# Two-layer gated cross-attention and mixture of experts: the first expert part cut to 16 tiles, and layer 0's experts started beside the last attention iterations

## The chip, the cores and the metric

The kernel runs on one core of a Trainium2 chip. The metric is the device time of one execution in microseconds (us), lower is better. The core has a matrix engine (PE), three elementwise engines (DVE, ACT, POOL) and a queue engine (SP) that only issues transfers; each engine works through its own list of instructions in order, and they meet at semaphores. A bank is one of eight 128 x 512 float32 blocks of PSUM, the memory that PE writes to.

## What is computed

Two layers over x, 128 sequences of 64 tokens of width 128 (8192 tokens, 64 tiles of 128). Each layer adds a cross-attention and then a mixture of experts, both gated by a tanh. What the change touches is in layer 0: a 16-head attention, then top-2 routing over 8 experts of hidden width 512.

```python
x = x + jnp.tanh(g_xattn[0]) * _L0_xattn_ref(_layernorm(x, axis=-1), ctx_1024, ctx_1024, ...)
x = x + jnp.tanh(g_ffn[0]) * _L0_ffn_ref(_layernorm(x, axis=-1), ...)
x = x + jnp.tanh(g_xattn[1]) * _L1_xattn_ref(_layernorm(x, axis=-1), ctx_1024, ctx_1024, ...)
x = x + jnp.tanh(g_ffn[1]) * _L1_ffn_ref(_layernorm(x, axis=-1), ...)

def _L0_ffn_ref(x, Wg, bg, W1, b1, W2, b2):      # E = 8, K = 2, H = 512
    scores = jax.nn.softmax(xt @ Wg + bg, axis=-1)
    topk_probs, topk_idx = jax.lax.top_k(scores, K)
    h = jnp.einsum('nd,edh->enh', xt, W1) + b1[:, None, :]
    h = jax.nn.gelu(h, approximate=False)
    eo = jnp.einsum('enh,ehd->end', h, W2) + b2[:, None, :]
    ...
    out = jnp.einsum('nk,nkd->nd', topk_probs, sel)
```

## The kernel before

**Stages.** Layer 0's attention is a software pipeline over NP = 32 pairs of tiles. Every engine has the loop `for p in range(NP + 3)`; iteration p scores pair p, turns the weights of pair p-1, attends for pair p-2 and writes the output of pair p-3. Its last three iterations (p = 32, 33, 34) only drain the pipeline. Then come layer 0's experts, layer 1's attention and layer 1's experts.

**Parts.** The expert layer works on three parts of the 64 tiles, `PARTS = ((0, 24), (24, 24), (48, 16))`. For each part DVE runs `route0(h)`, a generator of 12 steps (softmax, top 2, counts, where each token goes, which expert each block belongs to). DVE then normalises each tile's rows (`put_rows`), and POOL scatters them to DRAM with two indirect transfers for each tile (`put`), grouped by expert. A part becomes blocks of one expert each: first blocks of 256 rows, then 21 blocks of 128 rows. A part of 24 tiles has 17 + 21 blocks, one of 16 tiles 9 + 21, and all parts together have 43 large and 63 small blocks (NBL = 106). The rows of a large block, or of two small ones, are a unit.

**A block.** SP copies the expert's first weights (`fetch_weights`, three blocks ahead) and loads a unit's rows (`fetch_tokens`, three units ahead; it waits until the whole part is put). PE turns the rows (`turn0`, L837), multiplies by the first weights (`up0`, L847), ACT applies the gelu (L1752), PE multiplies by the second weights (`down0`, L857), DVE adds the bias (`add_bias0`, L1363) and SP stores the unit. When a part's last results are stored and every part's rows are put, POOL gathers the results, two indirect transfers a tile (`get`, L1960); DVE adds them to x (`combine`, L1371, in `earlier_part`), takes statistics, and POOL turns these into layer 1's means and scales (`moments1`). The gathers of the last part lie in layer 1's attention, where `LATER_BY` says how many tiles are combined by which group.

**Order around the change.** Part 0's `route0` begins at p = 17 and its scatters run from p = 23 to 34, two tiles an iteration; part 1's `route0` begins at p = 29; part 2's runs a step at a time between the first blocks of part 0. Scatters of parts 1 and 2 follow the loop, each tile behind its `put_rows`; DVE makes two rows a block while it is in part 0. Two fills of zeros (384 KB each, L459) go out in each iteration until 38 have. In the draining iterations PE, ACT and DVE also fold layer 1's weights (`turn_weights`, `output_bias(1)`, `multiply_weights`, `fold_weights`) in banks 0, 1 and 7. SP, behind all that it issues for the loop, fetches three blocks' weights, the two halves of `w2`, and the rows of units 0 to 2.

Of the kernel before, what the change touches and what calls it, by code (L numbers as in the profile page):

```python
# [13 lines left out]
ALU = mybir.AluOpType  # L14
# [6 lines left out]
P = 128  # L21
# [24 lines left out]
PARTS = ((0, 24), (24, 24), (48, 16))  # L46
# [39 lines left out]
PUT_FROM = 23  # L86
# [6 lines left out]


# [8 lines left out]
LATER_BY = (0, 1, 3, 5, 7, 9, 11, 13, 15, 16)  # L103
# [86 lines left out]
def build(nc, t_in, out):  # L190
    with ExitStack() as ctx:
# [30 lines left out]
        minus_half = sb("minus_half", [P, TS])  # L222
        ln_tmp = sb("ln_tmp", [P, 4, TS])
# [20 lines left out]
        xl_sb = sb("xl_sb", [P, P])  # L244
# [20 lines left out]
        scores_r = sb("scores_r", [P, 2, S])  # L265
        top = sb("top", [P, 2, 24])
        top_at = sb("top_at", [P, 2, 24], mybir.dt.uint32)
        tok = sb("tok", [P, 2, CAP])
        pair = sb("pair", [P, 2, CAP, 2])
        slot_sb = sb("slot_sb", [P, NCHUNK, NE, 2])  # L270
# [10 lines left out]


# [137 lines left out]
        def routing_start(h):  # L420
            return 2 * (sum(PARTS[h]) // TG - 1) + 7
# [8 lines left out]
        def sync_program(e):  # L430
# [46 lines left out]

            filling = fill()
            for p in range(NP):
                move_sums(p)  # L480
                if p % 4 == 2 and (p + 2) // 4 < NT // TS:
                    w.wait_ge(s_xl, (p + 2) // 4)
                    load_turned((p + 2) // 4)
                if p < NE:
                    load("w1", w1_sb[:, p, :], t_in["w1a"][:, p, :])
                for _ in range(2):
                    next(filling, None)
            for _ in filling:
                pass

# [28 lines left out]
            w.wait_ge(s_sc, NP)  # L519
            w.wait_ge(s_kx, NG)  # L520
            for b in range(AHEAD):
                fetch_weights(b)
            for i in range(2):
# [3 lines left out]
            for u in range(3):  # L527
                fetch_tokens(u)
# [50 lines left out]
        def tensor_program(e):  # L579
# [163 lines left out]
            def turn_weights():  # L743
                w.wait_ge(s_sub, NP)
                for n in range(3):
                    ins = e.transpose(banks[0][:, n * P:n * P + P], w_sb[:, 4 + n, :], ident[:])
                ins.then_inc(s_fm, 1)

            def multiply_weights():
# [4 lines left out]
                e.matmul(banks[1][:, 0:D], wk, wq, start=True, stop=True)  # L754
                e.matmul(banks[1][:, D:2 * D], wv, wo1_sb[:], start=True, stop=True)
                e.matmul(banks[1][:, 2 * D:2 * D + 1], wk, vec("bq1"), start=True, stop=True)
                e.matmul(banks[1][:, 2 * D + 1:2 * D + 2], wq, vec("bk1"), start=True, stop=True).then_inc(s_fm, 1)

            def multiply_bias():
                w.wait_ge(s_fs, 1)  # L760
                e.matmul(banks[0][:, 0:1], cen[:], fold1[:, 2:3], start=True, stop=False)
                e.matmul(banks[0][:, 0:1], ln_sb[:, ROUTER, 3, :], vec("bk1"), start=False, stop=True).then_inc(s_fm, 1)
# [20 lines left out]

            project_k(0)
# [1348 lines left out]
```

## Time and profile before

| | us |
|---|---|
| median of 3 runs (lowest to highest) | 1274.79 (1268.9 to 1282.43) |
| the profiled execution, its own time | 1269.73 |
| its span, first to last instruction | 1267.9 |
| granted TensorE clock, mean | 0.884 of full speed |

The span is what the views of the trace measure; the profiled execution's own time is 1.8 us more. By the lines that start and end in the trace, layer 0's attention takes the first 341 us, its experts the stretch to about 811, layer 1's attention to about 930, layer 1's experts the rest. In a view, a wait is put down to what ended it; "issue" and "remote" mean that no instruction of another engine is shown as having ended it.

### The profile page before, as it was taken

To read this page: it belongs to the slowest core of one execution; us is meant where nothing else is said; L and a number is where in the kernel's file an instruction comes from. 1 tells how busy PE (TensorE), PEld (TensorE's weight loads), DVE (VectorE), ACT (ScalarE), POOL (GpSimd) and SP (SyncE) were. 2 spreads that over 40 slices of the span, in tenths; PEclk is the share of its full clock that TensorE was granted. 3 is DMA by queue.
4 is the path that set the end of the run, shared out by engine and by line. 5 is a ranking of instruction groups with operands and counts; after the bars stand their busy time and mean duration, and the time that the engine had idled before them with its cause. 6 is when DMAs were issued, how large, how long until landed. Compare 5 with 4: busy or idle time off the path is not lost.

```text
span 1267.9 us, 25268 instructions
## 1 busy us (share of the span) xinstructions
PE 994.5 (78%) x8892; PEld 815.3 (64%) x8892; DVE 620.8 (49%) x1596; ACT 584.8 (46%) x1274; POOL 688.9 (54%) x909
## 2 busy tenths in 40 slices
PE   5999887886477828932999376967878999999993
PEld 2777765665356728912999276856756767677882
DVE  4899998676613413201462043557845343353331
ACT  2888865563132304401454034645544544544551
POOL 5655565584465371275022706365316766787886
PEclk9999999787678868955999578988989999999997
DMA  8454320111434423522545233521142636456444
GB/s 316 137 175 156 137 103 25 48 63 33 156 114 134 125 78 129 176 70 73 159 141 178 70 109 116 192 78 55 37 105 35 89 54 95 44 87 78 50 50 58
DMA packets 130813, 130.89 MB, mean 103 GB/s; under 512 B 33410, under 2 KB 103426, under 8 KB 129794
## 3 DMA queue, kind: packets, MB, share of 16 engines
q1 hardware_dynamic: 100466, 91.82, 23.1%
q0 software_dynamic: 28928, 29.91, 14.1%
q10 hardware_dynamic: 1296, 7.54, 1.5%
q8 instruction: 74, 1.21, 0.4%
q14 instruction: 49, 0.40, 0.1%
HBM read 54.01 MB, written 49.62 MB: 82 GB/s over the span
## 4 chain that ended last, share of the span: by engine, by line
PE 52%; another core or an unknown queue 14%; ACT 10%; DVE 10%; issue 6%; DMA 5%; POOL 2%; SPq 0%; POOLq 0%; DVEq 0%; ACTq 0%
PE psum L847 10%; PE psum L857 9%; PE psum L1015 7%; PE psum L1025 7%; PE psum L653 4%; ACT w_sb L1659 3%; PE psum L979 2%; DMA odd<-ln_sb,dest 2%; PE psum L680 1%; ACT work L1666 1%; PE psum L837 1%; PE psum L687 1%; DVE mx L1154 1%; DVE w_sb L1160 1%
## 5 line engine op out<-in xcount | busy, mean ns | idle before, releaser
L1752 ACT ACTIVATE hid_sb<-psum,work 128x128 f32<-128x128 f32 (+1 forms) x424 | 148.1, 411 | 311.0 <-remote 169.2
L847 PE MATMUL psum<-work 128*128 128x128 f32 (+1 forms) x848 | 175.2, 349 | 58.6 <-issue 46.1
L1960 POOL DMA_INDIRECT work<-yg,place x128 | 129.0, 1007 | 133.2 <-issue 109.7
L857 PE MATMUL psum<-w_sb,hid_sb 128*128 x1192 | 164.6, 286 | 31.2 <-issue 30.9
L847 PEld LDWEIGHTS psum<-work 128*128 128x128 f32 x848 | 135.0, 207 | 82.0 <-issue 66.5
L857 PEld LDWEIGHTS psum<-w_sb,hid_sb 128*128 128x128 f32 x1192 | 157.3, 203 | 35.4 <-issue 32.3
L1363 DVE TENSOR_TENSOR yg_sb<-psum,work 128x128 f32<-128x128 f32 (+1 forms) x106 | 36.5, 345 | 290.0 <-remote 153.9
L1015 PE MATMUL psum<-work,w_sb 128*128 128x272 f32 (+2 forms) x512 | 132.0, 399 | 4.2 <-ACT ctx_sb L1861 2.3
L2036 POOL DMA_INDIRECT out_x<-ln_sb,dest x68 | 106.1, 1560 | 45.4 <-DVE ln_sb L1579 27.1
L1861 ACT ACTIVATE ctx_sb<-psum,w_sb 128x272 f32<-128x272 f32 (+2 forms) x256 | 116.0, 488 | 26.2 <-PE psum L1015 21.6
L1025 PE MATMUL psum<-ctx_sb,w_sb 128*128 128x272 f32 (+2 forms) x512 | 128.0, 392 | 0.0
L2036 POOL DMA_INDIRECT odd<-ln_sb,dest x68 | 105.7, 1555 | 37.2 <-issue 18.3
L1015 PEld LDWEIGHTS psum<-work,w_sb 128*128 128x128 f32 x512 | 92.6, 190 | 31.5 <-ACT ctx_sb L1861 8.2
L1945 POOL DMA_INDIRECT xg<-work,place x80 | 78.4, 980 | 61.6 <-DVE work L1139 39.2
L1025 PEld LDWEIGHTS psum<-ctx_sb,w_sb 128*128 128x128 f32 x512 | 92.2, 190 | 15.4
L1894 POOL TENSOR_TENSOR ln_tmp<-stats 128x8 f32<-128x8 f32 (+1 forms) x33 | 8.7, 264 | 158.1 <-DVE stats L1071 137.1
L1666 ACT COPY work<-psum 128x512 f32<-128x512 f32 x128 | 69.9, 589 | 51.8 <-PE psum L653 44.9
L1917 POOL TENSOR_SCALAR work<-work,vec_sb 128x512 f32<-128x512 f32 x64 | 43.5, 697 | 82.6 <-ACT work L1643 67.8
L1564 DVE TENSOR_SCALAR work<-psum,b2T_sb 128x272 f32<-128x272 f32 (+6 forms) x96 | 36.1, 403 | 92.5 <-PE psum L1025 90.8
L1154 DVE TENSOR_REDUCE mx<-psum 128x32 f32<-128x2048 f32 x32 | 73.1, 2285 | 16.3 <-remote 10.5
L1827 ACT COPY work<-psum 128x272 f32<-128x272 f32 x64 | 24.8, 387 | 114.8 <-PE psum L979 112.6
L653 PE MATMUL psum<-ident,w_sb 128*128 128x128 f32 x512 | 76.9, 299 | 0.0
(240 smaller groups left out, 1812.3 us busy)
## 6 DMA issues: line engine op xcount, KB each, us to landing
work<-w_sb SPq DMA_DIRECT2D x76, 322.0 KB
work<-xg SPq DMA_DIRECT2D x73, 128.0 KB
yg<-yg_sb SPq DMA_DIRECT2D x73, 128.0 KB
xg<-yg_sb SPq DMA_DIRECT2D x24, 384.0 KB, 4.1
ctx_sb<-tok SPq DMA_DIRECT2D x8, 1088.0 KB
ctxn<-sums_sb SPq DMA_DIRECT2D x64, 64.0 KB
out_x<-x_sb SPq DMA_DIRECT2D x16, 256.0 KB
odd<-yg_sb SPq DMA_DIRECT2D x10, 384.0 KB, 3.1
```

Source lines behind the costliest of these rows:

```text
L653: ins = e.transpose(banks[B_T[half]][:, r * P:r * P + P], pr[:, i, pair // 2, u, 2 * (r % 2):2 * (r % 2) + 2, :], ident[:])
L847: e.matmul(banks[UP_BANKS[c]][:, 0:cols], w1g(b)[:, c * P:c * P + P], xgT_sb[:, u % 2, at:at + cols], start=True, stop=True).then_inc(s_up, 1)
L857: ins = e.matmul(banks[DOWN_BANKS[b % 2]][:, n * D:n * D + D], hid0[:, b % 2, c, n * P:n * P + P], w2_sb[:, bass.ds(number, 1), c, :].rear ...
L1015: e.matmul(banks[b][:, 0:m * SLOTS], w1_sb[:, ex, c * P:c * P + P], xgT[sg % 2][:, ex, 0:m, :].rearrange("p t s -> p (t s)"), start=True, ...
L1025: ins = e.matmul(banks[3][:, 0:SIZES[sg] * SLOTS], w2_sb[:, ex, c, :], hid[:, ex % 2, c, 0:SIZES[sg], :].rearrange("p t s -> p (t s)"), st ...
L1154: e.tensor_reduce(mx[:, p % 2, :], four_banks, AX_X, ALU.max).then_inc(s_mx, 1)
L1666: e.copy(pT[:, p % 2, u, 4 * half:4 * half + 4, :], banks[B_T[half]]).then_inc(s_pT, 1)
L1752: e.activation(hid0[:, b % 2, c, 0:cols], banks[UP_BANKS[c]][:, 0:cols], ACT.Gelu, bias=w1g(b)[:, HID + c:HID + c + 1]).then_inc(s_hg, 1)
L1861: e.activation(hid[:, ex % 2, c, 0:m, :].rearrange("p t s -> p (t s)"), banks[(HC * ex + c) % 3][:, 0:m * SLOTS], ACT.Gelu, bias=w1_sb[:, ...
L1945: e.indirect_dma_start(xg_dram[h], at, src, None, bounds_check=NROWS[h] - 1, oob_is_err=False).then_inc(s_put[i], 16)
L1960: e.indirect_dma_start(dst[:, k, :], None, yg_dram[h], at, bounds_check=NROWS[h] - 1, oob_is_err=False).then_inc(s_get[i], 16)
L2036: e.indirect_dma_start(sum_rows[n % 2], at, yr[:, n % RESULTS, i, :], None, compute_op=ALU.add, bounds_check=NT * P - 1).then_inc(s_add1[n ...
```

## The change

- The parts become 16, 28 and 20 tiles (`PARTS`). Blocks stay 43 large and 63 small: 9 + 21, 21 + 21 and 13 + 21.
- Part 0's routing begins at p = 12 and its scatters at p = 18, so that they end at p = 25; part 1's routing begins at p = 28. Three fills go out in each iteration instead of two.
- SP fetches the first three blocks' weights ahead of pair 30's sums, and the first half of `w2` and the rows of units 0 and 1 right behind them; the second half and unit 2 follow pair 31's sums.
- PE turns units 0 and 1 in iteration 32, does `up0(0)`, `turn0(2)` and `up0(1)` in iteration 33, and `down0(0)` in iteration 34, ahead of the last pair's output. DVE copies the turned rows there and makes four rows of part 1; ACT does the first two blocks' gelus in iteration 33. The block loops begin at b = 2.
- Layer 1's weights are folded between blocks 33 and 37 (`FOLD`), in bank 7.
- In part 1 DVE lets 17 blocks pass before the first `combine` (`UNTIL_ADDED`; it was 3). `LATER_BY` is stretched to 20 tiles. POOL's moments of layer 1 are placed anew, and the router's four calls become two of twice the width.
- Scratch tiles share memory to make room (`xl_sb`, `slot_sb`, `scores_r`, `pair`, `tok`).

```diff
-PARTS = ((0, 24), (24, 24), (48, 16))
+PARTS = ((0, 16), (16, 28), (44, 20))
-PUT_FROM = 23
+PUT_FROM = 18
+UNTIL_ADDED = (17, 3)
+FOLD = NBLK[0] + 3
-LATER_BY = (0, 1, 3, 5, 7, 9, 11, 13, 15, 16)
+LATER_BY = (0, 2, 4, 6, 8, 10, 12, 14, 16, 18, 20)
...
         def routing_start(h):
-            return 2 * (sum(PARTS[h]) // TG - 1) + 7
+            return -(-sum(PARTS[h]) // TS) * TS // 2 + 4
...
+            for p in range(NP):
+                if p == NP - 2:
+                    w.wait_ge(s_sc, NP)
+                    w.wait_ge(s_kx, NG)
+                    for b in range(AHEAD):
+                        fetch_weights(b)
+                move_sums(p)
...
+                for _ in range(3):
+                    next(filling, None)
+                if p == NP - 2:
+                    load_second(0)
+                    for u in range(2):
+                        fetch_tokens(u)
+            load_second(1)
+            fetch_tokens(2)
...
+                if p == NP + 2:
+                    down0(0, load_number(0))
...
                 if p == NP:
-                    turn_weights()
+                    w.wait_ge(s_pT, 4 * NP)
+                    turn0(0)
+                    turn0(1)
                 if p == NP + 1:
-                    output_bias(1, wo1_sb[:])
-                    multiply_weights()
-                if p == NP + 2:
-                    multiply_bias()
+                    w.wait_ge(s_sub, NP)
+                    up0(0)
+                    turn0(2)
+                    up0(1)
...
+            for b in range(2, NBL + 1):
...
+                if b == FOLD:
+                    output_bias(1, wo1_sb[:])
+                    turn_weights()
+                if b == FOLD + 2:
+                    multiply_weights()
+                if b == FOLD + 4:
+                    multiply_bias()
...
+                if p == NP + 1:
+                    stats_router(p - 3)
+                    for _ in range(sum(steps)):
+                        next(side, None)
+                    w.wait_ge(s_av, NP)
+                    for _ in range(TG):
+                        next(rows)
                 if 0 <= p - 2 < NP:
                     invert(p - 2)
...
+                if p == NP:
+                    copy_tokens(0)
+                    copy_tokens(1)
+                    for _ in range(sum(steps)):
+                        next(side, None)
+                if p == NP + 1:
+                    copy_tokens(2)
+                if p == NP + 2:
+                    add_bias0(0)
...
-                for _ in range(3):
+                for _ in range(UNTIL_ADDED[h]):
                     yield
-                for i in range(NLARGE[h + 1] - 3):
+                for i in range(NLARGE[h + 1] - UNTIL_ADDED[h]):
...
-                if t == PARTS[0][1] + 15:
-                    moments1(PARTS[0][1])
-            moments1(PARTS[0][1] + TS)
+                if t in (31, 39):
+                    moments1(t - 15)
             for t in range(PARTS[-1][0], NT):
                 get(t)
                 if t == PARTS[-1][0] + 1:
-                    moments1(PARTS[-1][0] - TS)
-            moments1(PARTS[-1][0])
-            for lo in range(0, NS, TS):
-                moments_router1(lo)
+                    moments1(32)
+                if t in (51, 57):
+                    moments1(40 if t == 51 else 48)
+            moments_router1(0, NS)
```

## Rows read from the trace of the kernel before

**Rows 1.** The page's busy time of each engine and its share of the span.
```profile
PE 994.5 (78%) x8892; PEld 815.3 (64%) x8892; DVE 620.8 (49%) x1596; ACT 584.8 (46%) x1274; POOL 688.9 (54%) x909
```
**Rows 2.** Stretches: bounds, length, busy us of each engine, clock, DMA share, GB/s.
```profile
26.00:182.00 156.00, 142.16 (x2809) 109.92 (x2809) 141.70 (x201) 124.92 (x215) 93.91 (x203) 0.99 0.41 140
...
543.00:595.00 52.00, 10.60 (x27) 6.82 (x28) 1.89 (x5) 1.90 (x4) 36.60 (x37) 0.50 0.22 62
```
**Rows 3.** Waits of ACT: line, what ended them, total us, times, longest.
```profile
ACT hid_sb L1752 <- remote: 169.2, 21, 40.2
```
**Rows 4.** Timeline of PE at whole speed: a large block, then two small ones.
```profile
601.72 1.89 PE L847 MATMUL psum<-work 128*128 128x256 f32 x8
...
605.45 1.89 PE L847 MATMUL psum<-work 128*128 128x256 f32 x8
...
499.36 1.06 PE L847 MATMUL psum<-work 128*128 128x128 f32 x8
...
503.15 1.06 PE L847 MATMUL psum<-work 128*128 128x128 f32 x8
```
**Rows 5.** Timeline of ACT: exponentials of pairs 11, 17, 22 and 31.
```profile
110.34 1.93 ACT L1659 ACTIVATE w_sb<-w_sb 128x2048 f32<-128x2048 f32 x1
...
155.28 1.94 ACT L1659 ACTIVATE w_sb<-w_sb 128x2048 f32<-128x2048 f32 x1
...
207.73 1.92 ACT L1659 ACTIVATE w_sb<-w_sb 128x2048 f32<-128x2048 f32 x1
...
312.87 1.90 ACT L1659 ACTIVATE w_sb<-w_sb 128x2048 f32<-128x2048 f32 x1
```
**Rows 6.** Timelines of DVE, SP, PE: last output, unit 0's load, blocks 0, 2.
```profile
340.98 0.48 DVE L1178 SCALAR_TENSOR_TENSOR x_sb<-psum,tg_sb,x_sb 128x256 f32<-128x256 f32 x1 [1.37 <-PE psum L687]
...
343.98 1.41 SPq L512 DMA_DIRECT2D work<-xg  x3
...
348.00 3.03 PE L847 MATMUL psum<-work 128*128 128x256 f32 x8
...
354.82 1.89 PE L847 MATMUL psum<-work 128*128 128x256 f32 x8
```
**Rows 7.** Timeline of POOL: part 1's first scatter, part 2's first and 28th.
```profile
348.44 1.12 POOL L1945 DMA_INDIRECT xg<-work,place  x1 [0.79 <-POOL nmr L1903]
...
440.59 0.97 POOL L1945 DMA_INDIRECT xg<-work,place  x1 [16.87 <-DVE work L1139]
...
475.14 0.97 POOL L1945 DMA_INDIRECT xg<-work,place  x1 [0.30 <-issue]
```
**Rows 8.** Timeline of PE: blocks 17 and 19, around part 2's scatters.
```profile
446.70 1.13 PE L847 MATMUL psum<-work 128*128 128x128 f32 x8 [0.38 <-issue]
...
481.15 1.92 PE L847 MATMUL psum<-work 128*128 128x128 f32 x8
```
**Rows 9.** Timelines: first and 46th gather of part 0; PE at blocks 38, 44.
```profile
529.51 1.06 POOL L1960 DMA_INDIRECT work<-yg,place  x1 [41.84 <-issue]
...
588.27 1.00 POOL L1960 DMA_INDIRECT work<-yg,place  x1 [0.30 <-issue]
...
520.21 1.89 PE L847 MATMUL psum<-work 128*128 128x256 f32 x8
...
596.39 3.49 PE L847 MATMUL psum<-work 128*128 128x256 f32 x8 [0.82 <-issue]
```
**Rows 10.** Timeline of PE, layer 1's attention: projections of three groups.
```profile
823.29 1.02 PE L888 MATMUL psum<-ctx_sb,w_sb 128*128 128x512 f32 x2
...
828.41 1.02 PE L888 MATMUL psum<-ctx_sb,w_sb 128*128 128x512 f32 x2
...
872.96 1.02 PE L888 MATMUL psum<-ctx_sb,w_sb 128*128 128x512 f32 x2
```
**Rows 11.** Timeline of POOL: a call of layer 1's moments, then the next gather.
```profile
764.94 0.21 POOL L1894 TENSOR_TENSOR ln_tmp<-stats 128x8 f32<-128x8 f32 x1 [34.14 <-DVE stats L1071]
...
770.48 1.16 POOL L1960 DMA_INDIRECT work<-yg,place  x1 [0.78 <-POOL nmr L1906]
```

More of the change, by code:

```diff
@@ L517, in store_results, with load_second @@
                 e.dma_start(rows, yg_sb[:, u % 3, 0:n, :]).then_inc(s_yg[u % 3], 16)
[L519 to L523, printed above, removed]
+            def load_second(i):
                 w.wait_ge(s_pt, 4 * (NP - 1 + i))
@@ L526, in sync_program @@
                 load("w2", w2_sb[:, half], t_in["w2a"][:, half])
-            for u in range(3):
-                fetch_tokens(u)
+            filling = fill()
+            for p in range(NP):
[5 more added lines that the diff above has]
+                move_sums(p)
+                if p % 4 == 2 and (p + 2) // 4 < NT // TS:
+                    w.wait_ge(s_xl, (p + 2) // 4)
+                    load_turned((p + 2) // 4)
+                if p < NE:
+                    load("w1", w1_sb[:, p, :], t_in["w1a"][:, p, :])
+                for _ in range(3):
[6 more added lines that the diff above has]
+            fetch_tokens(2)
             for b in range(NBL + 2):
@@ L782, in count0, with turn0, up0, down0 @@
                 free[B_P] = s_counted, h + 1
+            def turn0(u):
+                w.wait_ge(s_xg[u % 4], 16 * (u // 4 + 1))
+                w.wait_ge(s_xT, u)
+                for n in range(sum(m for _, m, _ in UNITS[u][2]) // P):
+                    ins = e.transpose(banks[4][:, n * P:n * P + P], xg_sb[:, u % 4, n, :], ident[:])
+                ins.then_inc(s_xt, 1)
+            def up0(b):
+                u, _, _, cols, at = BLOCKS[b]
+                w.wait_ge(s_xT, u + 1)
+                w.wait_ge(s_w1g[b % NW], 16 * (b // NW + 1))
+                for c in range(HC):
+                    n = HC * b + c
+                    w.wait_ge(s_hg, n - len(UP_BANKS) + 1)
+                    e.matmul(banks[UP_BANKS[c]][:, 0:cols], w1g(b)[:, c * P:c * P + P], xgT_sb[:, u % 2, at:at + cols],
+                             start=True, stop=True).then_inc(s_up, 1)
+            def down0(b, number):
+                cols = BLOCKS[b][3]
+                w.wait_ge(s_hg, HC * (b + 1))
+                w.wait_ge(ld["w2"], 32)
+                w.wait_ge(s_yb, b - 1)
+                for n in range(cols // P):
+                    for c in range(HC):
+                        ins = e.matmul(banks[DOWN_BANKS[b % 2]][:, n * D:n * D + D], hid0[:, b % 2, c, n * P:n * P + P],
+                                       w2_sb[:, bass.ds(number, 1), c, :].rearrange("p a d -> p (a d)"),
+                                       start=(c == 0), stop=(c == HC - 1))
+                ins.then_inc(s_dn, 1)
+            def load_number(b):
+                _, h, j, _, _ = BLOCKS[b]
+                w.wait_ge(s_expert, h + 1)
+                return e.value_load(expert[0:1, h, j:j + 1], min_val=0, max_val=NE - 1)
             project_k(0)
@@ L886, in project1 @@
             def project1(g):
+                w.wait_ge(s_fs, 1)
                 wait_bank(7)
@@ L1365, in add_bias0, with later_rows @@
                                 w1g(b)[:, HID + HC:W1].unsqueeze(1).to_broadcast([P, n, D]), ALU.add).then_inc(s_yb, 1)
+            def later_rows(first, last):
+                for t in range(first, last):
+                    put_rows(t)
+                    yield
+            rows = later_rows(PARTS[1][0], NT)
+            step.done(e.memset(hid_sb[:], 0.0))
+            units = hid_sb[:].rearrange("p (n c) -> p n c", c=32)
+            e.memset(units[0:S, :, ONES:ONES + 1], 1.0)
+            e.memset(units[S:P, :, HEAD_ONES:HEAD_ONES + 1], 1.0).then_inc(s_units, 1)
@@ L1367, in combine @@
+            for _ in side:
+                pass
             def combine(t):
@@ L1376, in combine @@
                 w.wait_ge(s_x2, t + 1)
-            def later_rows(first, last):
-                for t in range(first, last):
-                    put_rows(t)
-                    yield
             def statistics1(g):
@@ L1703, in softmax8, with up0 @@
                 yield
+            def up0(b):
+                cols = BLOCKS[b][3]
+                w.wait_ge(s_av, NP)
+                w.wait_ge(s_dn, b - 1)
+                for c in range(HC):
+                    w.wait_ge(s_up, HC * b + c + 1)
+                    e.activation(hid0[:, b % 2, c, 0:cols], banks[UP_BANKS[c]][:, 0:cols], ACT.Gelu,
+                                 bias=w1g(b)[:, HID + c:HID + c + 1]).then_inc(s_hg, 1)
             keys(0)
@@ L1762, in norm1 @@
                     ins.then_inc(s_ln1, 1)
-            for b in range(NBL):
+            for b in range(2, NBL):
                 up0(b)
+                if b == FOLD:
+                    turned_weights()
                 if b == 3:
```

239 lines of the change are left out of this document (89 added, 150 removed).

## The prediction

> **What bounds the kernel now.** I read the page, then busy time by stretches, then each engine's waits, then the timelines around the largest gaps. By the page no engine is busy all the time; PE has most at 78% [rows 1]. The stretches show two regimes. From 26 to 182 us layer 0's attention runs undisturbed, PE and DVE both busy some 142 of 156 us. From 543 to 595 us everything but POOL all but stands: PE 10.6, DVE 1.9, ACT 1.9, POOL 36.6 of 52 us, with the DMA engines at 0.22, so it isn't bandwidth [rows 2]. The waits say the same: ACT's gelus waited 169.2 us for nothing that the profile names [rows 3].
>
> The timelines show what lies beside these gaps. At whole speed a large block takes 605.45 - 601.72 = 3.73 us, two small ones with their turn 503.15 - 499.36 = 3.79, so 1.9 each [rows 4]. While POOL issues indirect transfers back to back, blocks don't come at that rate:
> - Part 2's first 28 scatters run from 440.59 to 476 us, one each 1.28 us [rows 7]. PE goes from block 17 to 19 in 481.15 - 446.70 = 34.5 us [rows 8], of which two small blocks are 3.8: 30.7 us lost, 1.10 for each scatter.
> - Part 0's 46 gathers run from 529.51 to 589.3, one each 1.31 us. PE goes from block 38 to 44 in 596.39 - 520.21 = 76.2 us, of which six large blocks are 22.4: 53.8 lost, 1.17 for each gather [rows 9].
> - Part 1's scatters begin at 348.44 [rows 7] and pause where DVE's next row is missing, so in shorter runs. From block 2 at 354.82 [rows 6] to block 17 at 446.70 [rows 8] are 91.9 us, of which 15 large blocks are 56.0: 35.9 lost, 0.75 for each of 48.
> - In the attention loop an iteration takes (155.28 - 110.34) / 6 = 7.49 us. From pair 22 to 31 nine take 105.1 instead of 67.4 [rows 5]: 37.7 lost over 36 scatters and half of part 1's routing.
>
> So a run of indirect transfers costs the other engines its own length less some 7 us of work that they had at hand. What keeps them is not shown; the idle time is called issue or remote, as if instructions or signals arrived late. The number of indirect transfers (256) doesn't change; where they lie, and in how long runs, does. That decides this change as much as the overlap in its name.
>
> [...]
>
> **The change part by part.** The sum is made against the profiled execution's own time, 1269.7 us, 5.1 under the median of 1274.8.
>
> 1. *The attention loop.* Part 0's routing cost 207.73 - 155.28 - 5 x 7.49 = 15.0 us [rows 5]. With 16 tiles for 24 only its wide steps shrink: 13, an estimate. Taking 7.5 for the half of part 1's routing, the 36 scatters cost 30.2, 0.84 each. The new loop holds 32, spread alike: 26.9. Of part 1's routing 7 steps of 12 fall in it, on 28 tiles: 9 instead of 7.5. Together 48.9 for 52.7: -4. The third fill a step is put at 0: DVE sets the pace, the DMA engines are at 0.41 [rows 2], and sums moved ahead of the fills wait only for those of the step before (bound: if it delayed each of 13 steps by 0.5, +6).
>
> 2. *The drain and the start of the experts.* Now the last output is at 340.98, unit 0's rows are asked for at 343.98 (behind part 0's last scatters), block 0 starts at 348.00 and block 2 at 354.82 [rows 6]. The drain from the last exponential's end, 314.8 [rows 5], to the last output's, 341.5, is 26.7 us. In the new one PE has two up0, one down0 and a turn ahead of the last output, some 9 us at the half clock that 3.03 us for an up0 stand for (1.89 at the whole one) [rows 4, 6]; unit 2's rows are behind a megabyte of w2 on SP's queue; DVE does the last routing steps and four rows ahead of its reciprocal. Taken out are the fold's products and PE's waits in them, some 5 us, an estimate. I take 26.7 + 9 - 5 = 31: last output at 341.5 - 4 + 4 = 341.5, and block 2 right behind, at 342. Block 2 comes 13 us sooner. Bounds: 5 (all nine and a late unit 2 added) and 20 (the nine hidden in waits for the sums' transfers).
>
> 3. *Scatters beside the blocks.* 12 of part 0's (two tiles in each of p = 32, 33 and 34) lay in the drain, where PE waited anyway. Now all of part 0's lie in the loop, and 96 instead of 80 lie beside blocks. The 80 cost 35.9 + 30.7 = 66.6, 0.83 each. If 96 cost the same, 80: +13. If all cost the 1.10 of the long run, 106: +39. For the upper side speaks that small blocks now begin at block 9, not 17: they get DVE's rows done sooner, so that POOL's runs are longer, and its pause of 16.9 us at 440.59 [rows 7] nearly closes, because part 2's routing is done sooner than part 1's 28 tiles are put. For the lower, that part 1's scatters begin beside large blocks as before. I take 0.9: 86.5, +20.
>
> 4. *Gathers beside the blocks.* They were 96, in runs of 48, 32 and 16; now they are 32 for part 0 and 56 for part 1 (32, 16, 8 by where the moments are placed). By 1.3 each less 7 a run: 104 before, 86 after, -18; by 1.17 each, -9. I take -15.
>
> 5. *A new wait.* POOL's moments1(16) comes ahead of get(32) and needs statistics that DVE takes right before combine(32). Such a call is 770.48 - 764.94 = 5.5 us [rows 11]; with two gathers and their landing some 10 from statistics to data. DVE waits in its queue, ahead of add_bias0, so PE runs out of a bank after two blocks: +5 (0 to 10). Before, the call lay four tiles ahead of the first missing one.
>
> 6. *The fold among the blocks.* PE and DVE hand over twice at block 33, some 2.5 us, plus the products: +3.
>
> 7. *Layer 1's attention.* 40 gathers instead of 32. A group took 5.12 us clear of them and six took 872.96 - 823.29 = 49.7 [rows 10]: 19 lost over 28 gathers, 0.68 each; eight more: +5 (0 to 9). The later moments and router calls have room until group 15's norm.
>
> Moved weights and scratch that shares memory cost nothing that I can find: SP is clear of its waits on scores when they come. Every term is left open by the bound beside it. Sum: -13 (with the -4 of step 1 in it) + 20 - 15 + 5 + 3 + 5 = **+5**, 1275 for this execution, and **1279** by the median.
>
> **Rivals.**
> 1. *Faster: the moved scatters cost nothing.* If block time, not POOL's runs, hides them, step 3 falls to 0, and the rest gives -15: 1260. For it: short runs cost less each. Against: neither long run was free [rows 8, 9]. It decides below 0.4 for each of the 96 scatters. 0.25.
> 2. *Slower: scatters and small blocks meet.* If POOL's runs close up, 96 lose 1.10 each, step 3 is +39 and the sum +24: 1299. It decides above 0.98 each. 0.24.
> 3. *The stalls don't follow POOL's transfers.* Steps 3, 4 and 7 fall away: -13 + 5 + 3 = -5, 1270. Rows 8 and 9 speak against it. 0.07.
> 4. *The early start doesn't come about.* If unit 2 or w2 is late and the last output with it, step 2 gives nothing: +18, 1293. 0.06.
>
> The forecast itself has 0.38, with a range of its own of 1266 to 1288.
>
> **How the numbers follow.** About 1% (12.7 us) is what a measurement of this kernel can tell from no change. Faster by more takes rival 1 mostly and a little of the forecast's low side: 0.27. Slower takes rivals 2 and 4 for the larger part: 0.27. The rest, with rival 3, is 0.46. The 80% range leaves out a tenth at either end: 1253 to 1300.
>
> **What would show it.** Block 2's up0 at 342 (335 to 350) tests steps 1 and 2. The loss from block 2 to the end of part 2's scatters, over 96, tests step 3: about 0.9, and POOL's pause between parts 1 and 2 under 8 us. Gathers of part 0 in one run of 32, starting at about 500. A wait of DVE at combine(32). Layer 1's attention some 5 us longer. The forecast is wrong if the new runs cost under 0.4 or over 1 each, or if block 2 isn't earlier.

## The result and the profile after

The changed kernel takes **1305.1 us**, the kernel before 1275.6 us (medians of four executions each); the ratio of the two is **1.023, 95% interval 1.017 to 1.028**: slower, where 1279 us and no measurable change were forecast. A later set of runs beside other runs of the kernel before gave 1309.5 us and 1.0275 (1.0248 to 1.0302); only this one has its whole interval above 2%. The first profile of the changed kernel was a disturbed one, so all rows of after are from the profile of a second run of the same kernel: span 1306.4 us against 1267.9, which is 38.5 us to explain. The medians differ by 29.5 and 31.7 us: the profiled execution of the kernel before (1269.7 us) lies 6 to 8 us under its medians, so some 8 of the 38.5 us are spread between executions, and the rows can't say which step they belong to.

The page's busy time: nothing is much busier than before [rows 1], so the 38 us are idle time.

```profile
span 1306.4 us, 25244 instructions
PE 1000.5 (77%) x8892; PEld 821.5 (63%) x8892; DVE 623.3 (48%) x1596; ACT 585.3 (45%) x1274; POOL 682.8 (52%) x891
```

The timelines answer [rows 5, 6, 7, 9, 10] step by step. ACT: the last exponential. PE: the turn of unit 0 with 7.38 us of idle time ahead of it, the last output (L697), block 2. POOL: part 1's first scatter, part 2's first, the last; then part 0's first gather. PE: the projections of layer 1's groups 0 and 15.

```profile
314.42 1.90 ACT L1696 ACTIVATE w_sb<-w_sb 128x2048 f32<-128x2048 f32 x1
...
327.40 0.66 PE L800 MATMUL psum<-ident,work 128*128 128x128 f32 x2 [7.38 <-DMA work<-xg]
...
346.73 0.63 PE L697 MATMUL psum<-wo_sb,ctxn 128*128 128x136 f32 x4
...
349.07 1.97 PE L810 MATMUL psum<-work 128*128 128x256 f32 x8 [0.38 <-issue]
...
353.69 1.17 POOL L1986 DMA_INDIRECT xg<-work,place  x1 [0.97 <-POOL nmr L1944]
...
448.60 0.97 POOL L1986 DMA_INDIRECT xg<-work,place  x1 [11.14 <-DVE work L1160]
...
504.96 0.97 POOL L1986 DMA_INDIRECT xg<-work,place  x1 [0.30 <-issue]
532.19 1.06 POOL L2001 DMA_INDIRECT work<-yg,place  x1 [26.25 <-issue]
...
839.57 1.02 PE L909 MATMUL psum<-ctx_sb,w_sb 128*128 128x512 f32 x2
...
955.72 1.02 PE L909 MATMUL psum<-ctx_sb,w_sb 128*128 128x512 f32 x2
```

For layer 1's two groups the kernel before has:

```profile
811.56 1.02 PE L888 MATMUL psum<-ctx_sb,w_sb 128*128 128x512 f32 x2
...
916.58 1.02 PE L888 MATMUL psum<-ctx_sb,w_sb 128*128 128x512 f32 x2
```

Time lost beside POOL's runs comes from windows of the up products alone: bounds, length, PE's busy us and (x) matmuls, the same for PEld, clock, DMA share, GB/s. Eight matmuls are a block; large blocks are worth 3.73 us and small ones 1.9 [rows 4]. First the kernel before from block 2 to the last scatter, then the changed one; then the changed one's gathers of part 0.

```profile
354.82:487.70 132.88, 45.04 (x160) 31.22 (x160) 0.78 0.36 113
```
```profile
349.07:505.90 156.83, 42.29 (x176) 31.39 (x176) 0.70 0.30 92
...
532.19:573.60 41.41, 10.92 (x26) 5.99 (x25) 0.69 0.34 92
```

Before: 160 matmuls are 20 blocks, 15 of them large, 65.5 us at whole speed: 67.4 of 132.9 us lost, 0.84 for each of 80 scatters. After: 22 blocks, 7 large, 54.6 us: **102.2 of 156.8 us lost, 1.06 for each of 96**.

The same windows split where part 2's scatters begin, the kernel before and then the changed one, say where the price rose:

```profile
354.82:440.59 85.77, 34.73 (x112) 22.95 (x112) 0.84 0.42 127
440.59:487.70 47.11, 10.31 (x48) 8.27 (x48) 0.67 0.27 86
```
```profile
349.07:448.60 99.53, 30.13 (x120) 22.11 (x120) 0.74 0.31 97
448.60:505.90 57.30, 12.15 (x56) 9.28 (x56) 0.62 0.27 85
```

Part 2's scatters cost 1.06 us each before (33.9 us over 32) and 1.10 after (44.0 over 40). Part 1's cost 0.70 before (33.5 over 48, beside 14 large blocks) and **1.04 after** (58.2 over 56, beside 7 large and 8 small ones). POOL's timeline shows what else changed there. A run ends where POOL stands for DVE's next row: before, part 1 goes out in runs of 16, 8, 8, 4, 8 and 4 scatters, and after in runs of 24, 8, 12 and 12. The first pause of each, before and after:

```profile
374.30 0.97 POOL L1945 DMA_INDIRECT xg<-work,place  x1 [5.57 <-DVE work L1139]
```
```profile
388.84 0.97 POOL L1986 DMA_INDIRECT xg<-work,place  x1 [4.62 <-DVE work L1160]
```

The prediction's terms beside what the two profiles show:

| steps | forecast | measured | from |
|---|---|---|---|
| 1 and 2, block 2's start | -13 | -5.8 | 349.07 - 354.82 |
| 3, scatters beside blocks | +20 | +34.8 | 102.2 - 67.4 |
| 4 to 6, gathers, new wait, fold | -7 | -1.0 | the rest of block 2 to group 0 (490.5 against 456.7) |
| 7, layer 1's attention, groups 0 to 15 | +5 | +11.1 | 116.15 - 105.02 |
| after group 15 | 0 | -0.6 | 350.7 - 351.3 |
| sum | +5 | +38.5 | |

### The profile page after: what moved, and what is told of

The parts are those of the page before. It is cut to its first block, busy times and chain, and to the rows that moved or that the text cites. A ratio compares the mean times of both kernels' runs of the same rounds, so it can differ in the third digit from the quotient of the medians.

```text
span 1325.7 us, 25244 instructions
## 1 busy us (share of the span) xinstructions
PE 1017.9 (77%) x8892; PEld 835.9 (63%) x8892; DVE 624.0 (47%) x1596; ACT 587.8 (44%) x1274; POOL 683.8 (52%) x891
## 4 chain that ended last, share of the span: by engine, by line
PE 48%; issue 13%; DVE 9%; another core or an unknown queue 9%; ACT 6%; DMA 5%; POOL 4%; SPq 4%; POOLq 0%; DVEq 0%; ACTq 0%
PE psum L810 11%; PE psum L820 10%; PE psum L1036 6%; PE psum L1046 6%; PE psum L1000 2%; SPq L480 2%; DMA odd<-ln_sb,dest 2%; DVE w_sb L1181 2%; DVE mx L1175 2%; PE psum L800 1%; PE psum L663 1%; ACT hid_sb L1749 1%; DMA work<-xg 1%; POOL odd L2075 1%
## 5 line engine op out<-in xcount | busy, mean ns | idle before, releaser
L1749 ACT ACTIVATE hid_sb<-psum,work 128x128 f32<-128x128 f32 (+1 forms) x424 | 150.9, 411 | 323.5 <-remote 167.6
L810 PE MATMUL psum<-work 128*128 128x128 f32 (+1 forms) x848 | 185.1, 363 | 88.9 <-issue 66.8
L810 PEld LDWEIGHTS psum<-work 128*128 128x128 f32 x848 | 143.9, 219 | 113.2 <-issue 93.6
L820 PE MATMUL psum<-w_sb,hid_sb 128*128 x1192 | 169.9, 293 | 22.9 <-issue 22.9
L820 PEld LDWEIGHTS psum<-w_sb,hid_sb 128*128 128x128 f32 x1192 | 163.5, 210 | 27.1 <-issue 24.1
L1935 POOL TENSOR_TENSOR ln_tmp<-stats 128x8 f32<-128x8 f32 (+2 forms) x31 | 8.3, 269 | 272.9 <-DVE stats L1092 208.5
L1986 POOL DMA_INDIRECT xg<-work,place x96 | 94.7, 986 | 58.5 <-issue 29.4
L1175 DVE TENSOR_REDUCE mx<-psum 128x32 f32<-128x2048 f32 x32 | 72.9, 2278 | 11.1 <-PE psum L651 7.8
```

The source lines that it names most:

```text
L810: e.matmul(banks[UP_BANKS[c]][:, 0:cols], w1g(b)[:, c * P:c * P + P], xgT_sb[:, u % 2, at:at + cols], start=True, stop=True).then_inc(s_up, 1)
L820: ins = e.matmul(banks[DOWN_BANKS[b % 2]][:, n * D:n * D + D], hid0[:, b % 2, c, n * P:n * P + P], w2_sb[:, bass.ds(number, 1), c, :].rear ...
L1175: e.tensor_reduce(mx[:, p % 2, :], four_banks, AX_X, ALU.max).then_inc(s_mx, 1)
L1749: e.activation(hid0[:, b % 2, c, 0:cols], banks[UP_BANKS[c]][:, 0:cols], ACT.Gelu, bias=w1g(b)[:, HID + c:HID + c + 1]).then_inc(s_hg, 1)
L1986: e.indirect_dma_start(xg_dram[h], at, src, None, bounds_check=NROWS[h] - 1, oob_is_err=False).then_inc(s_put[i], 16)
```

## The experiments

### The changed kernel again, and the change in halves

`after_again` is the changed kernel as it is. The two theories of the next texts: A, that the early start itself costs; B, that the new division into parts does. `parts_only` is the kernel before with the new division and what hangs on it:

```
-PARTS = ((0, 24), (24, 24), (48, 16))
+PARTS = ((0, 16), (16, 28), (44, 20))
-PUT_FROM = 23
+PUT_FROM = 18
...
-                for _ in range(2):
+                for _ in range(3):
                     next(filling, None)
...
+                if t in (31, 39):
+                    moments1(t - 15)
```

`parts_fold` moves the fold of layer 1's weights among the blocks as well, so that only the early start is missing from the change (one wait is added for the last pair's denominators, `w.wait_ge(s_lg, p)` at p = NP - 1). `fills3` has only the third fill.

> The changed kernel as it is, once more, for a profile that is not disturbed. Both theories: ratio 1.022 +- 0.004, about 1303 us. By the disturbed profile block 2 begins at 356.8 us (before 354.8), since the last exponential comes at 322.6 instead of 312.9. Theory A (the attention loop eats the early start) expects the last exponential still some 8 us later than before; theory B (the loss is beside the blocks only) expects it within 3 us of 312.9 and block 2 at 342 to 350.

> The kernel before with the new division into parts (16, 28, 20 tiles) and what follows from it alone: routing and scatters sooner, three fills a step, the new places of the moments. The experts still begin after the last tile and the fold stays in the drain. Theory B (the new division costs: more scatters beside blocks, worse gathers) expects 1.02 or more of before, about 1300 us or above, so that the early start is worth at most some us. Theory A (the early start itself costs) expects 1.00 to 1.007, 1275 to 1283 us.

> As parts_only, but with layer 1's fold among the blocks (33, 35, 37) as in the changed kernel, so that only the early start is left out of the change. Theory C (the fold among the blocks is the cost) expects it 10 us or more above parts_only. Theories A and B expect it within 5 us of parts_only; its difference from the changed kernel is the worth of the early start: 13 us by the prediction.

> The kernel before with three fills a step instead of two on SP's queue, nothing else. The prediction: 0 us, 1.000. Its bound: 6 us, 1.005, if each of 13 steps of the attention loop is delayed.

| kernel | median us | ratio to before | span | last exponential | first scatter beside blocks | last scatter | group 0 of layer 1 | its 16 groups |
|---|---|---|---|---|---|---|---|---|
| before | 1277.9 | | 1267.9 | 312.9 | 348.4 | 487.7 | 811.6 | 105.0 |
| fills3 | 1274.7 | 0.999 (0.996 to 1.002) | 1270.8 | 309.3 | | | | |
| parts_only | 1299.9 | 1.022 (1.016 to 1.027) | 1289.8 | 310.8 | 342.1 | 495.8 | 822.7 | 115.3 |
| parts_fold | 1297.2 | 1.019 (1.015 to 1.023) | 1292.3 | 314.8 | 341.9 | 492.6 | 828.4 | 114.4 |
| after_again | 1309.5 | 1.028 (1.025 to 1.030) | 1306.4 | 314.4 | 353.7 | 505.9 | 839.6 | 116.1 |

after_again came out at 1.028 for an expected 1.018 to 1.026; its last exponential (314.4) and block 2 (349.07) lie where theory B put them. Theory B holds for two thirds of the loss: the division alone costs 22 us (1.022). The fold among the blocks and the third fill cost nothing that these runs can tell. The early start, forecast at -13 us, costs some 12 (1309.5 against 1297.2, intervals apart; 8 against the 1305.1 of the first set, whose interval overlaps). Theory A had a cost of the early start, but the whole loss and in the attention loop. The two profiles say where: up to the last exponential parts_fold and the changed kernel are alike, and block 2 does come earlier, at 349.07 for 352.72:

```profile
341.86 1.11 POOL L1955 DMA_INDIRECT xg<-work,place  x1 [0.97 <-POOL nmr L1913]
...
342.75 0.66 PE L838 MATMUL psum<-ident,work 128*128 128x128 f32 x2 [7.23 <-DMA work<-xg]
...
352.72 1.89 PE L848 MATMUL psum<-work 128*128 128x256 f32 x8
```

But POOL's scatters start 11.8 us later (353.69) and end 13.3 later, and group 0 of layer 1 is still 11.1 us later. They also close up: part 1 goes out in runs of 24, 8, 12 and 12, where parts_fold has 12, 8, 8, 8, 8 and 12, since DVE's rows are ready when POOL comes to them. In POOL's queue they stand behind the moments of the last eight tiles, which need the last pair's output; and that output now has two up products, a down product and the turns ahead of it on PE. In parts_fold PE's last output is at 334.25, in the changed kernel at 346.73; 7.38 us of that are the wait for unit 0's rows.

### The new waits taken out one at a time

`moments_later` gives the gathers of tiles 32 to 35 their way past a statistics wait:

```
-                if t in (31, 39):
-                    moments1(t - 15)
+                if t in (35, 43):
+                    moments1(t - 19)
```

`tokens_first` asks for the rows of units 0 and 1 ahead of the sums of pair 30 and of w2 on SP's queue, and `scatters_first` puts eight scatters ahead of the last moments on POOL's:

```
+            for t in range(PARTS[1][0], PARTS[1][0] + TG):
+                put(t)
             moments(NT - TS, TS, s_st1, NT, s_momr)
-            for t in range(PARTS[1][0], NT):
+            for t in range(PARTS[1][0] + TG, NT):
                 put(t)
```

> The changed kernel with POOL's moments1(16) and moments1(24) four tiles later in its queue (behind the gathers of tiles 35 and 43 instead of 31 and 39), so that the gathers of tiles 32 to 35 wait for no statistics. Theory D (this call ahead of get(32) is a term of its own: with three rows of the division alone DVE waited 9.1 us and PE 7.3 us there) expects 7 us off, 1302 us, ratio about 0.995 of the changed kernel. Rival: the gathers only close up into one longer run, and the starved time grows by what the wait gave: 0.

> The changed kernel with the rows of units 0 and 1 asked for on SP's queue ahead of the sums of pair 30 and of w2 instead of behind them. In the changed kernel PE stands 7.4 us at 320 to 327 for unit 0's rows, with the last two pairs' attention behind the turn in its queue. Theory E (that wait delays the last output, the last statistics, and with them the 96 scatters and all that follows) expects 6 to 7 us off, about 1303 us. Rival F (nothing after the scatters' end moves, since the scatters are not what sets it): within 2 us.

> The changed kernel with the 8 scatters of tiles 16 to 19 ahead of POOL's call for the last statistics instead of behind it, so that they need not wait for the last pair's output. Theory P (the early products delay the last output, the last statistics and so part 1's scatters, from 341.9 us in parts_fold to 353.7, and that is why the early start gives nothing): 8 to 10 us off, about 1297 us. Rival: the scatters then starve the drain itself and the last output comes as much later: 0.

moments_later: 1312.0 us, 1.025 (1.017 to 1.033), against 1.023 and 1.028 of the changed kernel. The 7 us that theory D expects are 0.005, less than the interval, so the medians decide nothing; the profiles do better. In the changed kernel the wait is there as forecast in kind, DVE at combine(32) and PE behind it:

```profile
788.77 0.74 DVE L1410 SCALAR_TENSOR_TENSOR x_sb<-work,gate,x_sb 128x128 f32<-128x128 f32 x2 [9.15 <-DMA work<-yg,place]
...
790.12 0.66 PE L800 MATMUL psum<-ident,work 128*128 128x128 f32 x2 [7.03 <-issue]
```

In moments_later no wait of DVE for a gather is left there, but the 32 gathers ahead of it have become one run of 40 (689.3 to 741.2 us), and from the first gather to group 0 of layer 1 it takes 309.2 us (531.7 to 840.9) instead of 307.4. By this one profile the rival is right: what the wait gave went into a longer starved run.

tokens_first: 1307.5 us, 1.023 (1.018 to 1.028), **not decided**. From the last exponential to block 2 it takes 29.0 us instead of 34.7, but in its profile the last exponential came at 322.4 instead of 314.4, and a group of scatters had fallen one iteration later. The loop of the changed kernel shows both timings in the profiles taken of it and its variants, and I don't know what picks one.

scatters_first: 1301.7 us, 1.021 (1.016 to 1.025), span 1299.5, so 7 us under after_again's 1306.4; first scatter 342.9, last 495.4 (was 505.9), group 0 at 829.6 (was 839.6). Theory P, which expected 8 to 10 us, is borne out by the profile at 10 us up to group 0. The medians are weaker: 8 us under after_again with intervals that touch, and 3.5 under the first set's 1305.1.

### What one transfer costs, and what it is about them

`one_gather` leaves out the second gather of each tile, `plain_gather` replaces it by a plain transfer that POOL issues:

```
                 for k in range(TOP):
+                    if k == 1:
+                        e.dma_start(dst[:, k, :], yg_dram[h][P * (t % 16):P * (t % 16) + P, :]).then_inc(s_get[i], 16)
+                        continue
                     at = bass.IndirectOffsetOnAxis(ap=place[:, k, t:t + 1], axis=0)
```

> The kernel before with only one gather a tile instead of two (64 of 128 left out; the second expert's result is taken from the first one's rows, so the output is not the reference's, while DVE's work stays). Theory G (a run of indirect transfers on POOL's queue costs the others about its own length) expects 64 times 1.0 to 1.2 us less, of which those beside layer 1's attention 0.7: 55 to 70 us, about 1212 us. Rival H (the stalls do not follow the transfers): under 15 us.

> The kernel before with the second gather of each tile replaced by a plain transfer of 64 KB from consecutive rows, issued by POOL as well (wrong rows, so the output is not the reference's). If the cost is the indirect form's own work on POOL, about as one_gather, 1215 us; if it is any transfer issued by POOL, no change, 1276 us.

one_gather: 1197.7 us, 0.937 (0.931 to 0.943). 78.7 us for 64 gathers, **1.23 us each**, somewhat above the price that [rows 8, 9] gave (1.10 and 1.17) and above theory G's 55 to 70 us; it rules out rival H. The mean granted clock rose with it, from 0.884 to 0.911. plain_gather was forecast on two sides, 1215 or 1276, and hit neither: **1151.0 us**, 0.900 (0.894 to 0.906). It still issues 64 indirect gathers, and as many plain ones of the same size. POOL, then the windows (bounds, length, busy us of each engine, clock, DMA share, GB/s) of the gathers of part 0:

```profile
541.81 1.04 POOL L1963 DMA_INDIRECT work<-yg,place  x1 [0.30 <-issue]
542.85 0.57 POOL L1960 DMA_DIRECT2D work<-yg  x1
...
536.00:560.00 24.00, 23.44 (x165) 21.97 (x164) 8.76 (x24) 11.03 (x26) 20.36 (x25) 1.00 0.76 226
```

PE is busy 23.4 of 24 us at the whole clock, and the DMA engines move 226 GB/s. The same stretch of the kernel before:

```profile
529.50:589.30 59.80, 20.22 (x96) 15.76 (x94) 2.31 (x6) 4.27 (x10) 46.04 (x46) 0.60 0.28 79
```

So what starves the others here is not indirect transfers as such (in plain_gather they come 1.92 us apart) but indirect transfers that follow each other without a gap (1.30 us apart in the kernel before). The next kernels ask what the gap has to be. `paced_before` and `pace_one` put two or one small memsets, each waited for, behind every scatter and gather; `small_between` a plain transfer of 256 bytes; `small_per_tile` the same once a tile, behind the second of two:

```
                                          oob_is_err=False).then_inc(s_put[i], 16)
+                e.dma_start(small_dram[0, t, 0:1, :], ones_row[0:1, 0:64]).then_inc(s_small, 16)
```

and likewise in `get`. The memset kernels, which share scratch memory as the changed kernel does to make room, have inside the loop over the two transfers

```
+                    for _ in range(PAUSES):
+                        step.done(e.memset(pause_sb[:], 0.0))
```

> The kernel before with two small memsets of POOL (128x64, each waited for) behind every scatter and gather of layer 0, so that they come about every 1.9 us instead of 1.3, the spacing that they had in plain_gather, where nothing was starved. Theory I (what starves the others is the rate of POOL's indirect transfers): the starved time of all runs goes, 1150 us or less. Theory J (it takes a plain transfer between them): the runs only get longer and the others starve for longer, 1276 us or more.

> The kernel before with one plain transfer of 256 bytes (on-chip row of ones to a scratch row in memory) issued by POOL behind every scatter and gather. Theory J (a plain transfer between two indirect ones ends the starving, whatever its size): 1100 to 1150 us. Theory I: it depends on the spacing alone, the same here as in paced_before, since a plain issue took 0.6 us. If the 64 KB were needed (the indirect ones then waited for the DMA engines): 1276 us.

> The kernel before with one waited 128x64 memset behind every scatter and gather instead of two: spacing about 1.7 us instead of 2.12. Theory M (starving sets in only near the back-to-back rate of 1.3 us) expects PE busy in the runs and less waiting for landed rows: 1150 to 1180 us, below paced_before's 1228. Rival N (starving grows steadily with the rate): between 1228 and 1277.

> The kernel before with a plain 256-byte transfer behind every second indirect one (one a tile), mean spacing 1.6 us. If it is the mean rate that counts: as pace_one. If two indirect transfers back to back are enough to starve the others: above 1200 us.

| kernel | after each transfer | mean spacing us | median us | ratio to before |
|---|---|---|---|---|
| before | nothing | 1.28 to 1.31 | 1277.6 | |
| paced_before | two memsets | 2.12 | 1228.1 | 0.961 (0.956 to 0.966) |
| pace_one | one memset | 1.91 | 1182.7 | 0.930 (0.925 to 0.935) |
| small_between | a plain transfer | 1.87 | 1172.2 | 0.918 (0.913 to 0.922) |
| small_per_tile | a plain transfer after every second | 1.57 | **1109.3** | **0.873 (0.868 to 0.879)** |

The spacings are medians of the scatters, that of small_per_tile the mean of its two, 1.32 and 1.82; in runs of gathers they are 0.03 us longer. A memset does about as well as a plain transfer at about the same spacing (1182.7 at 1.91, 1172.2 at 1.87), so the gap counts, not its kind: theory J, which wanted 1276 us or more from memsets, falls. Theory I has the cause and not the time: paced_before was to reach 1150 us. At 1.6 us the windows below show no starving any more, and a wider gap makes POOL itself the bound: at 2.12 us DVE waits up to 52 us for gathered rows. Rival N falls with pace_one, which is 3 us above theory M's range. For small_per_tile both forecasts were too slow; two transfers 1.32 us apart and then 1.82 us to the next don't starve the others (PE busy 94% beside them). Rows of small_per_tile, then the windows of its scatters from part 1 on and of its gathers of part 0:

```profile
480.37 1.01 POOL L1963 DMA_INDIRECT work<-yg,place  x1 [0.30 <-issue]
481.38 0.54 POOL L1965 DMA_DIRECT2D small_rows<-ones_row  x1
482.23 1.04 POOL L1963 DMA_INDIRECT work<-yg,place  x1 [0.30 <-issue]
483.57 1.01 POOL L1963 DMA_INDIRECT work<-yg,place  x1 [0.30 <-issue]
...
337.30:467.20 129.90, 121.99 (x873) 114.07 (x874) 54.06 (x175) 61.63 (x170) 103.05 (x121) 0.98 0.59 180
467.60:542.60 75.00, 69.55 (x504) 64.74 (x503) 34.49 (x99) 32.03 (x86) 60.97 (x70) 1.00 0.66 177
```

PE is busy 94% and 93% of these stretches; in the kernel before it was busy 65% beside the scatters (85.9 of 132.9 us) and 34% beside the gathers. The 128 scatters, the 128 gathers and the computation are the same. This kernel beats both.

### Is it the starving that made the change slow?

If it were the starving alone, the change should be worth its early start once nothing is starved. Four kernels put the same gaps into the changed kernel, small_scatters_after behind its scatters only; small_scatters_before does that to the kernel before.

> The changed kernel with the same two memsets behind every scatter and gather. Theory I: 1150 us or less as well, and if the stalls were what made the change slow, not above paced_before: without them the early start is worth up to its 13 us. Theory J: 1310 us or more.

> The changed kernel with the same plain transfers of 256 bytes. If small_between is fast, this tells what the change is worth where nothing is starved: the early start's 13 us less the new waits for the moments, so 5 to 13 us under small_between; if the change's own waits (unit 0's rows, 7.4 us; the moments, 7 to 9 us; last statistics later) are what costs, the same or slower.

> The kernel before with the plain 256-byte transfers behind the scatters only; the gathers stay back to back. Theory K (the starved time of the scatters beside the blocks, 66 us here and 101 us in the changed kernel, is where the change lost) expects this at 1205 to 1215 us.

> The changed kernel with the same, behind the scatters only. Theory K: the two kernels' distance (28 us) falls by 35 us, to about -5, so 1200 to 1212 us. Rival L (with the starving gone its place is taken by a wait for part 1's rows, as with the transfers behind scatters and gathers: PE stood 35 us for them at block 30, because 30 blocks are over before 56 scatters are): the distance stays at 25 us or grows, 1235 us or more.

> The changed kernel with one plain 256-byte transfer a tile behind its two scatters or gathers. The kernel before with the same took 1109 us. Theory Q (the change's loss is POOL's scatters coming late and being more beside fewer blocks, whether the others are starved or not): 30 to 50 us above, 1140 to 1160 us. Theory R (the loss is the starving alone): 1090 to 1110 us.

| gaps | in the kernel before | in the changed one | the change costs |
|---|---|---|---|
| none | 1275.6 | 1305.1 | 30 |
| plain, scatters only | 1233.2 | 1260.4 | 27 |
| two memsets | 1228.1 | 1288.5 | 60 |
| plain, each | 1172.2 | 1229.2 | 57 |
| plain, every second | 1109.3 | 1161.7 | 52 |

Theory K, which was mine, falls: freed of the scatters' starving the change still loses 27 us, and freed of all of it nearly twice as much. Theory R falls too. The times are those of rival L (1235 us or more) and, 2 us past its range, of theory Q; small_between_after came out on the "same or slower" side. The profiles show where the distance lies (changed kernel less kernel before, us):

| gaps | up to the last exponential | from there to group 0 of layer 1 | the rest | span |
|---|---|---|---|---|
| none | +1.6 | +26.5 | +10.5 | +38.5 |
| plain, scatters only | +20.4 | -3.1 | +9.1 | +26.4 |
| two memsets | +22.3 | +15.3 | +21.4 | +59.0 |
| plain, each | +23.8 | +14.1 | +21.8 | +59.7 |
| plain, every second | +11.8 | +22.6 | +18.1 | +52.5 |

So 12 to 24 us of it are in the attention loop, which no theory had. There DVE waits for scatters to land before it reuses their four buffers: 32.9 us in small_scatters_after against 16.5 in small_scatters_before, as it was 18.5 against 4.5 without gaps. Why the loop of the changed kernel suffers more from the gaps is not shown; some 8 us may be its two timings. From the last exponential to group 0 the scatters-only pair's distance does fall, by 29.6 of the 35 us that theory K expected, and the loop takes 19 of them back. Rival L's wait is real all the same. PE in small_scatters_after and in small_between_after, at the turn of part 1's first unit:

```profile
469.55 0.69 PE L802 MATMUL psum<-ident,work 128*128 128x128 f32 x2 [38.50 <-DMA work<-xg]
```
```profile
472.09 0.69 PE L802 MATMUL psum<-ident,work 128*128 128x128 f32 x2 [35.38 <-DMA work<-xg]
```

Part 0 is now 30 blocks, 9 large and 21 small, 73 us at whole speed. Beside them POOL must issue 56 scatters for part 1; before, 38 blocks and 103 us covered 48 of them. At 1.9 us apiece 56 take 105 us, and PE runs dry. In small_per_tile_after (1.6 us) the same wait is 18.0 us. The other parts of its 52 us are the attention loop (last exponential 312.7 against 300.9; DVE waited 24.4 us for landed scatters against 11.0) and layer 1's attention (109.8 us against 91.9 for the 16 groups).

## Why the prediction was wrong

It put the bound in the right place (POOL's runs of indirect transfers, not bandwidth and not PE) and had the sign of each line of its table, but each of the four lines that carry the sum erred to the same side, by 6 to 15 us. The three misses of 6 and 7 us are no larger than the 8 us that one execution differs from the median; step 3's is.

- **Step 3 is the step that failed**: +34.8 for +20. The number of scatters beside the blocks (96 for 80) was right; the price was 1.06 us each, not 0.9. By the prediction's own account rival 2 decides above 0.98, and rival 2 (1299 us) is the case that came. Both of its reasons held in part 1: small blocks from block 9 on, and longer runs (24, 8, 12, 12 for 16, 8, 8, 4, 8, 4). What did not come is the closed pause ahead of part 2, still 11.1 us where under 8 were forecast. The mistake is to have priced the scatters by their number, with a mean over short and long runs, where step 4 prices by runs, each costing its own length less a constant. With 5.5 us for that constant (the two long runs of the kernel before give 5.1 and 6.5; "some 7" was too high) the rule makes the scatters' loss 59 us before and 88 after, an estimate: +29, most of the measured rise. What part the small blocks have in it no run tells.
- **Step 2**: block 2 at 349.07, just inside its 335 to 350, and 7 us later than 342. The wait for unit 0's rows, 7.38 us, now stands in the middle of the drain, in front of the last two pairs' attention in PE's queue. The prediction had looked at unit 2's rows and at w2 on SP's queue, not at unit 0's: they are asked for behind the sums of pair 30. Worse, it forecast the last output unmoved and followed nothing behind it: DVE's last output came 6.4 us later (347.39 for 340.98), and with it the last statistics in POOL's queue and part 1's scatters behind them, 353.69 for 348.44. Without the early start they begin at 341.86 (parts_fold), and put ahead of the statistics at 342.89 (scatters_first). Step 2's gain was spent by the time step 3 began. Its 3.03 us for an up0 were read as the half clock; the granted clock in that stretch was 0.62.
- **Step 1**: -4 forecast, +1.6 measured (last exponential 314.42 for 312.87). Three kernels with the loop of before but for a third fill in one of them (fills3, one_gather, plain_gather) had it at 309.3, 315.6 and 315.4, so this is within the spread; no saving shows.
- **Steps 4 to 6**: -7 for -1.0. The run of part 0's gathers is 32 as forecast and starts at 532, not at 500: it waits for part 0's last results, and PE comes to part 1's first block only at 530.7. The new wait was there (DVE 9.2 us, PE 7.0 us for a forecast of 5), but by moments_later's profile it is no term of its own: taken out, its time goes to a longer run. The fold cost nothing that could be told, for +3.
- **Step 7**: +11.1 for +5. Eight more gathers at 0.68 were probably too cheap by the same error as in step 3: one_gather puts a gather at 1.23. But that isn't all: with nothing starved the 16 groups still took 17.9 us more (109.8 for 91.9), and no run takes the eight gathers and the new places of the moments apart.
- **Rival 3** (the stalls don't follow POOL's transfers) is ruled out by one_gather (78.7 us less for 64 gathers) and small_per_tile (1109.3 us for the same transfers with gaps). The prediction's "as if instructions or signals arrived late" is not shown: no run tells what the starved engines lack. In the 51 us from 537 to 588 of the kernel before, the view of its DMA queues lists no packet of the two instruction queues, which moved 123 over the whole span; but PE did only 44 matmuls there and DVE and ACT 4 instructions each, so that is open. **Rival 4** was half true: the early start came about and gave nothing.
- **Rival 1**'s bound was wrong: its step 3 of 0 is 66.6 / 96 = 0.69 us for each scatter, and 1% faster is reached at 0.72, not at 0.4.
- The range (1253 to 1300) ended 1 us above rival 2, which alone had a chance of 0.24. The upper bounds of all terms together (-5 + 39 - 9 + 10 + 3 + 9) are +47, or 1322 us.

What the prediction did not ask, and what the gaps show, is whether the scatters are a bound in another way: 56 scatters at 1.28 us are 72 us of POOL alone, as long as the 30 blocks (73 us) that were to hide them.

## What to carry to other kernels

When a part of a pipeline is cut smaller to start sooner, count what must be issued for the next part while it runs, queue by queue, and follow the moved work into each queue that waits on its last result: here a block 6 us earlier went with scatters 5 us later. A mean price per transfer that is read from runs with pauses in them did not hold when the pauses moved (0.70 us for each of part 1's scatters before, 1.04 after); price by runs, or take the price of the longest one as the bound. And where all engines crawl while one issues transfers back to back, try a gap between them before moving anything: one 256-byte plain transfer behind every second one was worth 12.7% here, five times what the change under study lost.

## What the runs showed of the hardware

Beside indirect transfers that POOL issued back to back, one each 1.31 us, PE was busy 34% of the stretch shown, ACT 7% and DVE 4%, and the DMA engines moved 79 GB/s at a share of 0.28. Beside gathers at a mean of 1.6 us PE was busy 93%, ACT 43% and DVE 46%, and they moved 177 GB/s at a share of 0.66. A memset made the gap about as well as a plain transfer did: 1182.7 us at a spacing of 1.91 us, 1172.2 us at 1.87. How little gap would do, between 1.3 and 1.6 us, and what the starved engines lack was not tried. TensorE's mean granted clock was 0.957 of full speed in small_per_tile, against 0.884 before, and 0.60 in the starved stretch shown; what part of the gain this is was not measured.
